# Segment sums and basis products of a two-layer GNN megakernel: order of base groups, zero products at flushes, load order, one-hots on ScalarE

## The reference, cut to what matters

```python
def rgcn_gate_layer(x, row, col, edge_type, basis, att, gate_w, root, bias):
    w = jnp.einsum('rb,bio->rio', att, basis)        # 30 bases of 512 x 512, 2 relations
    x_j = x[col]
    msgs = []
    for r in range(NUM_RELATIONS):
        gate = jax.nn.sigmoid(x_j @ gate_w[r, :, 0])
        msgs.append(gate[:, None] * x_j @ w[r])
    msg = jnp.where((edge_type == 0)[:, None], msgs[0], msgs[1])
    agg = jax.ops.segment_sum(msg, row, num_segments=x.shape[0])
    return agg + x @ root + bias

h = jax.nn.relu(rgcn_gate_layer(x, row, col, edge_type, basis1, att1, gate_w1, root1, bias1))
out = rgcn_gate_layer(h, row, col, edge_type, basis2, att2, gate_w2, root2, bias2)
# beside it: qkv = xn @ W_qkv, q and k through elu + 1, KV = k^T v, out = q KV / (q sum k), @ W_out
```

## Time and profile before

| | |
|---|---|
| median of 3 runs | 995.76 us (995.1 to 997.72) |
| the profiled execution's own time | 1000.76 us |
| its span in the trace | 999.0 us |
| PE busy | 920.8 us (92%) |
| DVE busy | 621.9 us (62%) |
| ACT busy | 400.4 us (40%) |
| mean granted clock of PE | 0.966 of full |

### The profile page before, as it was taken

How to read it: one execution, slowest core, us unless ns; L and a number is a source line. 1 busy time by engine, 2 the same in 40 slices (tenths; PEclk the granted TensorE clock), 3 DMA queues, 4 the chain that set the end, 5 groups by cost and what they waited for, 6 DMA issues and landing times. The chain is left out here.

```text
span 999.0 us, 12275 instructions
## 1 busy us (share of the span) xinstructions
PE 920.8 (92%) x4532; PEld 610.8 (61%) x4532; DVE 621.9 (62%) x1272; ACT 400.4 (40%) x670; POOL 112.4 (11%) x98
## 2 busy tenths in 40 slices
PE   4689888969989999999998999989999899999997
PEld 1255544555444494469666655989997644545885
DVE  6589989847787771331304762698777533658861
ACT  4479866311102210111112342378885543423550
POOL 0000000000030204100002000143330000023300
PEclk9789889979999999998999999999999999999899
DMA  8898968585640362044786202312102100230001
GB/s 295 315 353 291 348 235 317 202 286 181 204 154 0 117 192 84 1 169 147 270 308 190 91 1 67 107 44 85 43 2 97 72 0 4 88 84 1 1 1 52
DMA packets 63839, 137.31 MB, mean 137 GB/s; under 512 B 6096, under 2 KB 20052, under 8 KB 63763
## 3 DMA queue, kind: packets, MB, share of 16 engines
q1 hardware_dynamic: 62642, 134.95, 39.0%
q0 software_dynamic: 1120, 1.29, 0.5%
HBM read 132.84 MB, written 3.38 MB: 136 GB/s over the span
## 5 line engine op out<-in xcount | busy, mean ns | idle before, releaser
L415 PE MATMUL PS<-AR 128*125 128x512 f32 (+9 forms) x1394 | 394.0, 440 | 11.0 <-DVE AR L1436 2.8
L415 PEld LDWEIGHTS PS<-AR 128*128 128x128 f32 (+3 forms) x1394 | 212.4, 194 | 171.0 <-issue 162.0
L1978 ACT ACTIVATE AR<-PS 128x500 f32<-128x500 f32 (+6 forms) x73 | 41.8, 577 | 169.1 <-PE PS L415 79.6
L1981 ACT ACTIVATE AR<-iota,AR 125x625 f16<-125x625 f16 x119 | 86.1, 809 | 30.4 <-PE PS L500 30.4
L1393 DVE SCALAR_TENSOR_TENSOR AR<-spare,cst,AR 128x512 f32<-128x512 f32 x96 | 69.6, 780 | 24.5 <-DMA spare<-in_rest 24.5
L498 PE MATMUL PS<-AR 125*125 125x512 f16 (+9 forms) x425 | 66.9, 319 | 5.3 <-issue 3.1
L1282 DVE TENSOR_SCALAR AR<-iota,AR 125x625 f16<-125x625 f16 x165 | 60.5, 443 | 12.6 <-PE PS L500 12.6
L498 PEld LDWEIGHTS PS<-AR 125*125 125x125 f16 x425 | 49.9, 151 | 26.8 <-issue 16.3
L447 PE MATMUL PS<-AR 128*32 128x512 f32 x276 | 44.6, 657 | 15.0 <-DMA AR<-in_basis 13.3
L550 PE MATMUL PS<-Dr,GXh 125*128 125x314 f32 (+1 forms) x160 | 48.0, 317 | 10.7 <-DVE AR L1398 9.7
L2474 POOL TENSOR_TENSOR whl<-AR,whh 128x512 fp32r<-128x512 f32 x32 | 47.4, 1500 | 90.2 <-ACT whh L1978 90.2
(11 more groups left out here) (321 smaller groups left out, 1493.7 us busy)
## 6 DMA issues: line engine op xcount, KB each, us to landing
AR<-in_basis SPq DMA_DIRECT2D x46, 768.0 KB, 8.5
spare<-in_rest SPq DMA_DIRECT2D x48, 512.0 KB, 4.3
AR<-in_L_ffn_W SPq DMA_DIRECT2D x20, 1024.0 KB, 7.6
spare<-in_basis SPq DMA_DIRECT2D x18, 768.0 KB, 8.2
AR<-in_L_gnn_Wh SPq DMA_DIRECT2D x8, 512.0 KB, 3.9
AR<-in_L_gnn_Wh SPq DMA_DIRECT2D x16, 256.0 KB, 4.6
AR<-in_L_mix_W_qkv SPq DMA_DIRECT2D x1, 3072.0 KB, 14.0
AR<-in_L_gnn_root SPq DMA_DIRECT2D x2, 1024.0 KB, 17.3
```

The source lines that it names most:

```text
L415: ins = te.matmul(o, l, r, start=start and i == 0, stop=stop and i == len(pairs) - 1)
L1978: return se.activation(o, i, ACT.Copy, scale=scale)
L1981: return se.activation(o, i, f, bias=bias, scale=scale)
```

## The change

Five edits in one. (1) Base group 1 moves from ahead of segment 0 to behind segment 1, and every later one moves by two segments; groups 12 and 13 stand behind segments 22 and 23. DVE's `combo_in(1)` moves with it. (2) In the flushes after segments 5, 11 and 17, two zero products of 512 columns stand on PE ahead of each bank product but the first; ahead of `root1` stand eight, which wait for the first of the last flush's five DVE instructions. (3) In odd segments ACT makes six of the seven source matrices, DVE one. (4) SP's queue: `Wqkv` in four parts, with rest pieces 3 and 4 between them; R2 behind piece 14, R1 and the small tables behind piece 19; pieces 35 to 37 behind the gate weights of layer 2. (5) DVE's adds are spread differently: four behind each `z_out`, one inside each of the first nine `phi`, four behind the last q unit and the last k/v unit.

```diff
-AFTER = [g // 2 + 2 if g % 2 else None for g in range(NS)]
+AFTER = [g // 2 + 1 if g % 2 else None for g in range(NS - 2)] + [12, 13]
...
-            return range(u, min(u + BY_ACT, v))
+            return range(u, min(u + BY_ACT + g % 2, v))
...
-            combos(1)
...
                     for k in range(7):
+                        if g and k:
+                            for _ in range(2):
+                                te.matmul(PS[0:P, 0:512], zer[0:P, 0:P], zer[0:P, :], start=False, stop=False, skip_group_check=True)
                         if g:
                             pe.wait_ge(flush_done, NT * (g // PER - 1) + min(NT, (512 * k + 511) // N + 1))
...
             pe.wait_ge(d_r1e, 64)
+            pe.wait_ge(flush_done, NT * (FLUSHES - 1) + 1)
+            for _ in range(8):
+                te.matmul(PS[0:P, 0:512], zer[0:P, 0:P], zer[0:P, :], start=True, stop=True, skip_group_check=True)
...
-            pe.wait_ge(d_wqkv, 16)
+            pe.wait_ge(d_wqkv, 64)
...
-            combo_in(1)
...
-                    add_rest(6 if kc == 1 or r == 0 else 4)
+                    add_rest(4)
...
                 ve.tensor_scalar(t, i, 0.0, None, ALU.min).then_inc(phi_min, 1)
+                if phis.n < 9:
+                    add_rest(1)
                 dv.wait_ge(phi_exp, phis.next()[1])
...
-                add_rest(2 if m < 3 else 5)
+                add_rest(2 if m < 3 else 4)
...
-                add_rest(6 if c < 4 else 8)
+                add_rest(6 if c < 4 else 4)
...
+            def load_qkv(k):
+                ye.dma_start(Wqkv[:, k, :], A["L0_mix_W_qkv"][128 * k:128 * k + 128, :]).then_inc(d_wqkv, 16)
...
-            ye.dma_start(Wqkv, kp(A["L0_mix_W_qkv"])).then_inc(d_wqkv, 16)
+            load_qkv(0)
+            load_qkv(1)
+            load_rest(3)
+            load_rest(4)
+            load_qkv(2)
+            load_qkv(3)
+            for q in range(5, 15):
+                load_rest(q)
+            ye.dma_start(R2, kp(A["L0_gnn_root2"])).then_inc(d_r2, 16)
+            for q in range(15, 20):
+                load_rest(q)
             ye.dma_start(R1, kp(A["L0_gnn_root1"])).then_inc(d_r1, 16)
-            ye.dma_start(R2, kp(A["L0_gnn_root2"])).then_inc(d_r2, 16)
...
-            for q in range(3, 36):
+            for q in range(20, 35):
```

More of the change, by code:

```diff
@@ L2557, in _ @@
             load_gates(1, d_gw1)
-            for q in range(36, 39):
+            for q in range(35, 38):
                 load_rest(q)
@@ L2576, in load_more @@
                     ye.dma_start(EXP2[i], kp(A["L0_ffn_W2"][bass.ds(e, 1), :, :].rearrange("o k n -> (o k) n"))).then_inc(d_e2[i], 16)
-            for q in range(39, VLOADS):
+            for q in range(38, VLOADS):
                 load_rest(q)
```

## The result

| | before | changed |
|---|---|---|
| median | 996.74 us (995.1 to 1000.96, 4 runs) | 982.17 us (981.15 to 984.86, 4 runs) |
| profiled execution, its span | 1000.76, 999.0 us | 984.86, 982.8 us |
| PE, DVE, ACT busy | 920.8, 621.9, 400.4 us | 922.7, 619.9, 407.7 us |

What follows compares the result with a forecast made beforehand. PE (busy 920.8 of 999.0 us) bounds the kernel, DVE sets the pace in the segment stage. Terms -12.0 - 1 - 11.3 - 1.9 + 0.5 + 0.8 = -24.9 give a median of 970.9 us, range 964 to 983.

Steps and rivals of the forecast that it cites:

- Step 1: Start of the segments: segment 0 can run at once, DVE's whole stage -11.1 us, `combo_in(1)` +1.3.
- step 4: Last segments: base group 12 +2.7 us, zero products behind group 13's loads +1.4; `root1` starts at 153.1, -12.0.
- Step 2: Odd segments 3 to 21: one source matrix moves from DVE to ACT, -3.3 us; worth nothing if ACT were late.
- Step 3: Three flushes: zero products hold the clock, -3 us, between 0 and -6.6; +3 x 0.86 if it falls anyway.
- Rival A: Flushes and `root1`: the zero products don't hold the clock, 6.6 us more, 977.5; chance 0.12.
- step 5: `root1`: the zero products may save the loss at the low clock, -1 us, from 0 to -1.7.
- Rival B: Segment stage: every group waits for its ring loads, `root1` at 163, -12 becomes -2, 980.9; chance 0.12.
- Step 6: z units: eight without a hole take 23.5 us, so q comes sooner, -11.3 us, allowed -8 to -11.3.
- Step 7: Ahead of the KV sums: four fewer DVE adds shorten PE's wait for copies, -1.9 us, from -2.5 to 0.
- Step 8: Given back later: R1 and tables delay adds in k/v units, +0.5 us; more adds in second layer's z units, +0.8.
- rival C: k/v units: SP's tables take 15.8 us again, piece 20 lands 8 us later, 978.4; chance 0.11.
- The rule weighed against term 3: Flushes: they hold no long idle gaps, so short zero products change nothing and the sum would be -18.3.

Runs made afterwards that it cites:

- experiment 5: `no_flush_zeros` with edit 1 undone (old order of the base groups): 982.2 us, 0.9853 of the kernel before.
- experiment 9: `five_onehots`, set against `no_flush_zeros`: 977.25 us, 0.9812 against 0.9796 of the kernel before.
- no_flush_zeros: The changed kernel without the zero products in the three flushes, the eight ahead of `root1` kept: 978.81 us, 0.9796 of the kernel before.
- segments: The changed kernel with edits 4 and 5 undone, so edits 1 to 3 only: 995.78 us, 0.9982 of the kernel before.
- experiments 6 and 8: `spread_groups` and `spread_no_zeros`, both with the base groups spread otherwise: 977.29 us, 0.9806, and 980.97 us, 0.9852.
- experiments 7 and 8: `no_zeros` and `spread_no_zeros`, both without any of the added zero products: 978.5 us, 0.9805, and 980.97 us, 0.9852.
- spread_no_zeros: The changed kernel without any added zero products and with the base groups spread over the segments: 980.97 us, 0.9852 of the kernel before.
- no_zeros: The changed kernel without any of the added zero products, flushes and `root1` alike: 978.5 us, 0.9805 of the kernel before.
- spread_groups: `no_flush_zeros` with the base groups spread evenly, group 12 two segments ahead of group 13: 977.29 us, 0.9806 of the kernel before.
- five_onehots: `no_flush_zeros` with edit 3 undone (no sixth source matrix on ACT): 977.25 us, 0.9812 of the kernel before.
- loads_alone: The kernel before with edit 4 only (SP's order), the adds as before: 994.21 us, 0.9969 of the kernel before.
- loads_adds: The kernel before with edits 4 and 5 only (SP's order and the spread adds): 983.92 us, 0.9867 of the kernel before.
- adds_alone: The kernel before with edit 5 (spread adds) and pieces 35 to 37 behind the gate weights, SP's queue otherwise as before: 990.38 us, 0.9948.

## Why the prediction was right in range and wrong in its middle

**Step 1, the start: right, though later than forecast.** PE was ready at 25.39 and its first products ran from 28.08 (26 to 27 was forecast), at the low clock: 3.98 us for its 14 products with the window at 0.50. DVE went on at 32.20 instead of 29.3. The first flush was 11.3 us early. The forecast's -11.1 + 1.3 = -9.8 us for DVE's whole stage needs the kernels without flush zeros to be seen: there the lead is 9.6 us in the means at flush 1 and still at flush 3, and the last segments and group 13 then take half of it, as step 4's +2.7 and +1.4 said. Edit 1 is worth 3.4 to 5.7 us (experiment 5).

**Step 2, source matrices: 1.6 us by the ratios for 3.3, and not told from nothing.** In experiment 9's traces flush 4 is no sooner with the edit (153.07 against 151.31), and DVE's waits for PE are 3.9 us longer. The step's own rival ("if ACT were late") does not show in them: DVE's waits for ACT differ by 0.8 us.

**Step 3, flushes: most likely the wrong sign.** I took -3 with bounds of 0 and -6.6 if the clock held. It held in five of the six flushes of the changed code that were traced, and in none of `no_flush_zeros`, and the zeros still cost: 0.9852 with them, 0.9796 without, 5.6 us by the ratios, with intervals that overlap a little. The working that failed is "0.65 of the 0.71": it took 0.216 us for the bank product and for the zeros as in a row of equal products, and the step is 0.93. Six steps of 0.93 are 5.6 us where DVE's instructions give the banks free within 3.67. The segment behind a flush then starts 1.8 to 2.8 us later at the full clock (changed kernel and `segments`), not 0.86, and that uses up what the full clock gives back. Rival A had the price for a clock that falls anyway, not for one that holds.

**Step 4, the last segments: `root1` at 165.78 for 153.1.** This is where the error shows, -12.0 against +0.7 in the two traces and about -1.8 for the whole of edits 1 to 3 by `segments` (0.9982). I had let DVE set the pace because it worked for 113.57 of 128.35 us. PE's share of that stage I had not set beside it: 112.10 us, nearly as much. By the ratios the error of edits 1 to 3, about 11 us, is step 3's in the main: 8.6 us (+5.6 for -3), step 2's 1.7 (-1.6 for -3.3) and step 5's 1 or so, with nothing left for edit 1. Each of these ratios is uncertain by 3 to 4 us, so that they add up so well is partly chance. The traces agree in kind: with the flush zeros 3.8 us of the lead are lost by flush 3 and 1.7 more by flush 4. The +2.7 for base group 12 was right, 2.8 in the means. From the end of the last flush to `root1` it is 3.5 us in the changed kernel (162.26 to 165.78) for the 1.7 of the sum (151.4 to 153.1), group 13's loads being later than I put them. That the stage lost time because two busy engines take turns was my explanation at first; the traces without flush zeros speak against it as the cause of the lost lead. Rival B (the ring sets the pace) holds at one place only: group 13's four waits cost 6.6 - 2.7 = 3.9 us, PE waited for the ring at no other group of the segments, and taking these waits away (experiments 6 and 8) lowered no median.

**Step 5, `root1`:** 13.90 for 15.67 us, -1.8 for -1. Whether the zero products did it is open: four of six traces without them have the short form too (experiments 7 and 8).

**Step 6, z units: right.** -11.6 for -11.3, hole gone, DVE's largest wait for a piece there 1.07 us. The cause I named, SP's queue, is only half of it: it needs edit 5 too.

**Step 7, KV:** -1.5 for -1.9. **Step 8, given back:** the tables' eight issues took 4.2 us in all (238.85 to 243.02 in SP's queue), near the 4 us that I took, so rival C did not come; from q to the end the span fell by 3.5 us, 1.5 of it the KV wait, where I had expected to pay 1.3. That stretch takes from 769.6 to 775.1 us in the nine traces with the changed loads and adds, so the other 2.0 us may be nothing but the spread.

**The rule weighed against term 3.** The sum by the rule of the Trainium skill, page "TensorE: Matmul & The Clock Gate", section "HAM oscillation" (avoid single long idle gaps, so these zeros change nothing), was nearer to the measurement than mine, but not for its reason: with the zeros the clock did hold in two flushes here, and in all three of `segments`, where it had fallen before. And in the changed kernel's second it fell, at about 91 us, with PE busy for the whole of the last 3 us and no idle piece in its flush longer than 0.45 us. Neither this section of the Trainium skill nor its section on depth-cycling foretells both.

**Luck in the range.** The range held because its upper part was there for the rivals, and none of A, B and C came as written. Of the signs that the prediction named, those of the z units and the KV wait came true and that of the start nearly (28.08 for 26 to 27), while the last flush (158.59 for 149 to 154), the clock behind the second flush and the start of q (210.78 for 197 to 202) did not.

Left open: what the flush zeros cost beside the longer flush and the fall at 91 us, and whether they cost as much as the ratios say, since the two intervals overlap; why one zero product of two was no better than both; why `spread_no_zeros` came out above `no_zeros` (intervals overlap by 0.0013); why the loads and the adds together bring about 5 us more than the sum of each alone; and what made the clock fall in the second flush of one execution and not of another. The best version measured here is the change without its flush zero products: 0.9796 to 0.9812 in four forms (`no_flush_zeros`, `no_zeros`, `spread_groups`, `five_onehots`), 977 to 979 us, which can't be told apart.

## What to carry to other kernels

When two engines hand buffers to each other, read the busy share of both in the stretch before calling one the bound (here 87 and 88%). A lighter load on one may then come back as its waiting time, and the sum of its waits (here 10.9 against 7.0 us for 3.3 us of work) is where to look. Follow a head start from milestone to milestone, in more than one trace: here it lasted until the other engine got more to do. Filler products belong only where the engine waits anyway for longer than they take, by the start-to-start time of that very mix of products. A late transfer and the work that is queued between two waits on it belong together: here either edit alone brought a quarter to two fifths of what both did.

## What the runs showed of the hardware that I had not expected

A product of one row and 512 columns with two zero products of 125 rows between it and the next took 0.93 us from start to start at the full clock, 0.35 of it from the bank product to the first zero, and 1.66 at the low one. The clock fell in a flush in which PE was busy throughout (3.00 of the 3 us ahead of 91 us), and held in the same flush of `segments`, which has the same code. Behind the wait of 2.44 or 2.45 us ahead of `root1` it held in `loads_alone`, `loads_adds` and `spread_no_zeros`, and was at the low level in the kernel before and in `adds_alone` (0.50 from 166 to 168 and from 163 to 165 us). And the same segment code put `root1` at 159.4, 162.3, 162.5 and 165.1 us in four executions.
